# A five-engine graph-network kernel: every engine's round in another order, and another table of PSUM banks

## The chip, the cores and the metric

One core of one Trainium2 chip. The metric is the device time of one execution in microseconds; a smaller one is better. All data is fp32.

## The reference, cut to what matters

128 graphs with 128 nodes and 256 features each go through four residual layers. Every layer normalises x, applies relu, and adds its result to x:

```python
# L0, hypergraph convolution, twice, with a layer norm between; H = (adj != 0)
m = Be[:, :, None] * einsum('nce,nch->neh', H, x @ W1.T);  h = Dn[:, :, None] * einsum('nce,neh->nch', H, m)
h = layer_norm(relu(h + b1));  y = hypergraph_conv(h, adj, W2, b2);  y + x
# L1, graph attention: softmax over nodes of where(adj > 0.5, leaky(Wh1 + Wh2.T), -9e15), times Wh, then elu
# L2, three diffusion hops: transition = A*exp(leaky(sj + si)) / rowsum;  H = sum_k (transition^k X) Wk + bk; relu
# L3: w = softmax over nodes of rowsum((q k^T) * adj);  w * v
h = relu(layer_norm(x)); x = x + L0(h, adj);  ... x = x + L1(...);  x = x + L2(...);  x = x + L3(...)
```

## The kernel before

Four graphs form a group, and there are 32 groups. The kernel is a software pipeline over groups. In round i, group i+1 is prepared ("next": degrees, scaled incidence), group i goes through L0 and L1 ("front"), group i-1 through L2 ("mid"), group i-2 through most of L3 ("late"), and group i-3 is finished and stored ("tail"). Rounds 1 to 35 are the same function `body`; rounds 6 to 30 run as a hardware loop. Round 0 has its own list, `opening`.

Each engine has a `body` of its own, which is a list, written out by hand, of small named blocks. The order of the list is the order in which that engine works; between engines only semaphores count. A block waits for its inputs (`wait_ge`), and, where it writes a PSUM bank that another block used, for the reader of the old content (the calls of `wait` at a block's head).

TensorE's blocks of a round, in the order before: `front_w1(0)`; `front_att` 0 and 1, `mid_az` 2 and 3, `front_att` 2 and 3 of the round before; `front_w1` 1 and 2; `late_ak`; the transposes `mid_h2(0)`, `front_w1(3)`, `mid_h2(1)`; then `mid_p2` 0 to 3 mixed with the high passes `front_w2` and followed by `front_w2_low` and `front_sums`; `mid_b2`, `late_h3(0)`, `mid_p10` 0 and 1, `front_c2`, `tail_turn`, `next_s`, `mid_p10` 2 and 3, `late_h3(1)`, and then `late_vqk`, `mid_ap`, `next_d`, `front_b1`, `next_y`, `mid_az` and `front_mix`. Products of weights run in three passes of a split format (high times high, and two with the low parts); each block of six matmuls is one group of four graphs or one chunk.

ScalarE evacuates PSUM: `copy_u` (two activations for each of four chunks, hT and its high part), `elu_exp`, `relu_p0`, `copy_h2T`, `copy_p2`, `copy_p10`, `exp_edges`, `copy_vqk`, `tail_exp`. VectorE does the layer norms (`mid_ln2`, `late_ln3`, `front_ln1`: statistics, aggregation, subtraction), the low parts (`mid_low`, `late_low`, `front_low`, `y_low`), `mid_columns` (which writes sij from the last columns of the four p2 products), `front_variance`, `front_z`, `front_residual`, `next_degrees` (its last step, L1387, writes deg), `front_dots`, and the softmax steps. GpSimd does the adds that only touch SBUF and the power -0.5 of every variance (`rsqrt`). SP issues the DMAs in its own order: the loads of x and of the adjacency, the copy of the mask, the store.

`BANK` gives the PSUM banks (0 to 7, 512 fp32 columns each) of every named product: `"u": (1, 2, 0, 3)` puts the first chunk of u into bank 1. `late_ak(past)` works for the group of the round before, `tail_sum` to `tail_out` form the softmax over nodes by two small transpositions, `tail_row` and `tail_turn`.

## Time and profile before

| | us |
|---|---|
| median of 3 runs | 1414.67 (1414.25 to 1416.06) |
| profiled execution, its own time | 1416.56 |
| its span, first to last instruction | 1414.6 |

Busy time in the span: TensorE (PE) 1368.1 us, VectorE (DVE) 1270.0, ScalarE (ACT) 1053.9, GpSimd (POOL) 949.0. PEclk is the granted share of TensorE's clock; it is 1.00 in steady rounds and 0.985 in the mean over the span. Times in the rows are microseconds from the span's start. Matmuls are pipelined: the recorded end of one lies behind the start of the next, so the pace is read from start to start. The round shown in the rows begins for TensorE at 394.77 with `front_w1(0)`.

### The profile page before, as it was taken

How to read it: one execution, taken by the hardware profiler on the slowest of the kernel's cores; microseconds unless marked ns; L12 is line 12 of the kernel's file. 1: busy time of each engine (PE TensorE's matmuls, PEld its weight loads, DVE VectorE, ACT ScalarE, POOL GpSimd, SP SyncE). 2: the span in 40 equal slices, each digit the busy share in tenths (PEclk: the TensorE clock that was granted, in tenths of full speed). 3: DMA queues.
4: the chain of work that ended last, by engine and by line, in shares of the span. 5: the costliest groups of instructions: out<-in, count | busy, mean ns of one | idle time of the engine just before them, and what ended most of it. 6: DMA issues, size and time to landing. Idle time of an engine off the chain costs nothing.

```text
span 1414.6 us, 33539 instructions
## 1 busy us (share of the span) xinstructions
PE 1368.1 (97%) x8924; PEld 1249.5 (88%) x8924; DVE 1270.0 (90%) x5265; ACT 1053.9 (74%) x2345; POOL 949.0 (67%) x974
## 2 busy tenths in 40 slices
PE   7789999999999999999999999999999999999985
PEld 6678999999999999999999999999999999999975
DVE  6869999999999999999999999999999999999883
ACT  4556777877777887777887777788777788777664
POOL 5647666667766666866666776666686666677533
PEclk9889999999999999999999999999999999999997
DMA  4100111101111101111110111110111111011001
GB/s 127 31 28 27 38 38 54 53 24 44 52 37 52 52 23 46 50 52 37 52 46 28 44 52 37 52 52 22 44 52 52 37 52 44 30 44 37 31 31 53
DMA packets 75383, 62.15 MB, mean 44 GB/s; under 512 B 3013, under 2 KB 70985, under 8 KB 75338
## 3 DMA queue, kind: packets, MB, share of 16 engines
q1 hardware_dynamic: 75338, 61.63, 13.7%
q8 instruction: 19, 0.31, 0.1%
q14 instruction: 26, 0.21, 0.0%
HBM read 36.45 MB, written 16.78 MB: 38 GB/s over the span
## 4 chain that ended last, share of the span: by engine, by line
PE 92%; DVE 5%; issue 2%; ACT 1%; DMA 0%; POOL 0%; POOLq 0%; DVEq 0%; ACTq 0%; SPq 0%
PE ps L357 39%; PE ps L342 25%; PE ps L361 19%; PE ps L463 4%; PE ps L418 3%; DVE stats L1321 1%; DVE prod L1505 1%; DMA x_in<-in_x 0%; PE ps L619 0%; DVE h L1333 0%; DVE x L1468 0%; PE ps L615 0%; DVE x L1416 0%; DVE z L1461 0%; DVE el L1406 0%
## 5 line engine op out<-in xcount | busy, mean ns | idle before, releaser
L1100 POOL TENSOR_TENSOR x3n<-p,x 128x512 f32<-128x512 f32 x64 | 82.2, 1285 | 260.7 <-ACT p L853 260.7
L1060 POOL TENSOR_TENSOR hT_lo<-hT,hT_hi 128x512 fp32r<-128x512 f32 x126 | 161.3, 1302 | 56.8 <-ACT hT L795 42.1
L1040 POOL TENSOR_TENSOR rs<-var_e,neg_half 128x4 f32<-128x4 f32 x160 | 165.2, 1033 | 23.7
L774 ACT ACTIVATE p<-ps,rs 128x256 f32<-128x256 f32 (+1 forms) x256 | 136.6, 597 | 27.9 <-DVE sij L1422 27.6
L357 PE MATMUL ps<-wl_hi,h2T_hi 128*128 128x512 f32 (+1 forms) x512 | 148.5, 372 | 0.7 <-DVE x L1468 0.7
L342 PE MATMUL ps<-p,alT 128*128 128x256 f32 (+1 forms) x512 | 143.4, 383 | 0.5 <-DVE p L1446 0.5
L357 PE MATMUL ps<-wl_lo,h2T_hi 128*128 128x512 f32 (+1 forms) x512 | 132.3, 340 | 0.0
L361 PE MATMUL ps<-wl_hi,h2T_lo 128*128 128x512 f32 (+1 forms) x512 | 131.8, 339 | 0.0
L1321 DVE BATCH_NORM_STATS2 stats<-x 128x6 f32<-128x256 f32 x256 | 108.8, 425 | 5.7
L871 ACT ACTIVATE h3T_hi<-ps 128x512 fp32r<-128x512 f32 x64 | 38.3, 598 | 90.8 <-PE ps L463 86.9
L795 ACT ACTIVATE hT_hi<-ps,cols_sb 128x512 fp32r<-128x512 f32 x128 | 87.4, 683 | 21.8 <-PE ps L361 21.6
L361 PEld LDWEIGHTS ps<-wl_hi,h2T_lo 128*128 128x128 f32 x512 | 88.1, 190 | 11.6
L357 PEld LDWEIGHTS ps<-wl_lo,h2T_hi 128*128 128x128 f32 x512 | 88.4, 190 | 10.9
L1113 POOL TENSOR_TENSOR p<-p,bk 128x512 f32<-128x512 f32 x64 | 81.9, 1279 | 21.1 <-ACT p L774 21.1
L795 ACT ACTIVATE hT<-ps,cols_sb 128x512 f32<-128x512 f32 x128 | 87.5, 683 | 8.4 <-PE ps L361 4.8
L342 PEld LDWEIGHTS ps<-p,alT 128*128 128x128 f32 x512 | 85.1, 192 | 5.6 <-DVE p L1446 0.8
L1505 DVE CUSTOM_DVE_ANT_0 prod<-va,ps 128x256 f32<-128x256 f32 x256 | 90.0, 417 | 0.0
L357 PEld LDWEIGHTS ps<-wl_hi,h2T_hi 128*128 128x128 f32 x512 | 83.1, 191 | 6.4 <-issue 1.1
L1075 POOL TENSOR_TENSOR x<-x 128x512 f32<-128x512 f32 x64 | 80.6, 1281 | 11.7 <-ACT x L774 11.7
L463 PE MATMUL ps<-ident,h 128*128 128x128 f32 x512 | 79.4, 277 | 7.1 <-DVE h L1333 7.1
L357 PE MATMUL ps<-w_hi,hT_hi 128*128 128x258 f32 x512 | 85.8, 290 | 0.0
L357 PE MATMUL ps<-yT_hi,w_hi 128*128 128x512 f32 x256 | 85.4, 414 | 0.0
(188 smaller groups left out, 4604.9 us busy)
## 6 DMA issues: line engine op xcount, KB each, us to landing
x_in<-in_x SPq DMA_DIRECT2D x32, 512.0 KB, 3.4
out_x<-x SPq DMA_DIRECT2D x32, 512.0 KB, 3.2
adj_f<-in_adjT SPq DMA_DIRECT2D x32, 256.0 KB, 2.7
adj_m<-in_adjT SPq DMA_DIRECT2D x32, 256.0 KB, 2.9
adj_l<-adj_m SPq DMA_DIRECT2D x32, 256.0 KB, 2.4
vqk<-in_l_wk SPq DMA_DIRECT2D x3, 256.0 KB, 4.9
x<-in_w1T SPq DMA_DIRECT2D x1, 512.0 KB, 6.7
x<-in_w2T SPq DMA_DIRECT2D x1, 512.0 KB, 7.6
```

Source lines behind the costliest of these rows:

```text
L342: last = pe.matmul(dst, lhsT(c), rhs(c), start=(c == 0), stop=(c == chunks - 1))
L357: pe.matmul(dst, lhsT(a, c), rhs(b, c), start=(a == b == c == 0), stop=False)
L361: last = pe.matmul(dst, lhsT(1 - late, c), rhs(late, c), start=False, stop=(c == chunks - 1))
L463: last = pe.transpose(bank(name, b)[:, ((g % 2) * KC + c) * P:((g % 2) * KC + c + 1) * P], h[:, g, c * P:(c + 1) * P], ident[:])
L774: return act.activation(dst, src, ACT.Copy, scale=scale)
L795: act.activation(dst[:, hc, :], bank("u", hc), ACT.Relu, bias=cols_sb[:, 0, hc:hc + 1]).then_inc(S[ready], 1)
L1040: pool.tensor_tensor(rs[:, layer, :], var_e[:, layer, :], neg_half[:], ALU.pow).then_inc(done, G)
L1060: pool.tensor_tensor(hTs[1][:, hc, :], hT[:, hc, :], hTs[0][:, hc, :], ALU.subtract).then_inc(S["hT_lo"], 1)
L1100: pool.tensor_tensor(x3n[:, s], p0[:, s], x2[:, s], ALU.add).then_inc(S["x3_ready"], 2)
L1113: pool.tensor_tensor(p0[:, s, :], p0[:, s, :], bk[:].rearrange("p (a d) -> p a d", a=1) .broadcast_to((P, 2, D)), ALU.add).then_inc(S["p0b ...
L1321: dve.bn_stats(stats[:, layer, g, :], src[:, g, :]).then_inc(st, 1)
L1505: dve.tensor_tensor_reduce(prod[:, k, :], va[:, k * D:(k + 1) * D], bank("hp", b)[:, (g % 2) * D:(g % 2 + 1) * D], 1.0, 0.0, ALU.mult, ALU ...
```

## The change

Every engine's list is put into another order. No block is added, dropped or given to another engine. The table of banks is new, and with it the waits at the blocks' heads, since these belong to the bank's former user. In the opening, constant rows go to other banks accordingly.

TensorE: `mid_h2(0)` runs ahead of `late_ak`; the order among `mid_p2` and `front_w2` is other, with `mid_p2(3)` later; `tail_row` moves behind `late_h3(0)`; `next_s` moves ahead with `tail_turn` between its halves; `late_h3(1)`, `late_vqk` 0 and 1 and `next_d` run ahead of `mid_p10(3)`. ScalarE: `elu_exp(0)` and `relu_p0(1)` move from behind the next round's `copy_u(0)` to ahead of it; `tail_exp` moves behind `copy_h3T(0)`, `copy_s` ahead of `norm_x`, whose second half comes much later. GpSimd: `mask_edges` and both `add_bias` move behind the next round's `add_res0(0)`. VectorE: the counts and `binc` run ahead of `next_moments`, `tail_max` behind `front_variance`, `tail_sum` directly behind `tail_weights`. SP: `load_adj` and `store` ahead of `load_x`.

The diff, cut to its core:

```diff
-        BANK = {"u": (1, 2, 0, 3), "y": (1, 4), "s": (3, 4), "d": (2,), "c2": (5, 0), "b1": (0, 3), "att": (3, 5),
-                "h2": (7, 6), "p2": (4, 5, 6, 7), "p10": (6, 7, 5, 0), "b2": (4,), "z": (0, 1, 2, 3),
-                "ap": (4, 5, 6, 7), "az": (5, 4), "h3": (5, 7), "vqk": (3, 1, 2, 0), "ak": (1,),
-                "row": (2,), "turn": (1,), "yA": (3, 2), "hp": (2, 6)}
+        BANK = {"u": (1, 3, 0, 2), "y": (1, 3), "s": (4, 5), "d": (6,), "c2": (0, 7), "b1": (3, 2), "att": (2, 7),
+                "h2": (4, 6), "p2": (4, 5, 6, 7), "p10": (7, 5, 3, 7), "b2": (6,), "z": (0, 1, 2, 3),
+                "ap": (4, 5, 6, 7), "az": (5, 6), "h3": (4, 1), "vqk": (5, 4, 0, 2), "ak": (3,),
+                "row": (5,), "turn": (2,), "yA": (4, 0), "hp": (2, 0)}
...
             def load_x(r):
-                wait(sp, S["h0_ready"], r.front(G))
                 wait(sp, S["xb_ready"], r.front(G))
+                if not r.steady and r.i == 0:
+                    wait(sp, S["h0_ready"], r.front(G))
                 sp.dma_start(x_in[:], group(x, r.i + 1)).then_inc(S["x_loaded"], 16)
...
@@ -317,12 +316,13 @@
             def body(r):
                 past = r.later(-1)
                 if r.has_next:
+                    load_adj(r)
+                if past.has_tail:
+                    store(past)
+                if r.has_next:
                     load_x(r)
-                    load_adj(r)
                 if past.has_mid:
                     hand_adj(past)
-                if past.has_tail:
-                    store(past)
                 if past.has_front:
                     load_mask(past)
...
@@ -468,7 +463,9 @@
...
-                if g == 2:
+                if g == 0:
+                    wait(pe, S["h2T_lo"], r.mid(2))
+                elif g == 2:
                     wait(pe, S["h2T_lo"], r.mid(G))
                 pe.wait_ge(S["h2T_copied"], r.mid(2 * (g // 2) + 2))
...
@@ -480,22 +477,19 @@
...
                 if g == 0:
-                    wait(pe, S["p2_copied"], r.mid(3))
+                    wait(pe, S["p2_copied"], r.mid(G))
                 elif g == 1:
-                    wait(pe, S["p2_copied"], r.mid(G))
-                elif g == 2:
-                    wait(pe, S["x1_ready"], r.front(2))
-                    if not r.steady and r.i == GROUPS:
-                        wait(pe, S["h3T_lo"], r.late(2))
+                    wait(pe, S["wex_ready"], r.tail(G))
                 elif g == 3:
-                    wait(pe, S["x1_ready"], r.front(G))
+                    if not r.steady and r.i == GROUPS - 1:
+                        wait(pe, S["x1_ready"], r.front(G))
...
@@ -509,9 +503,10 @@
...
                 if g == 2:
-                    wait(pe, S["wex_ready"], r.tail(G))
+                    if not r.steady and r.i == 0:
+                        wait(pe, S["hT_ready"], r.front(G))
                 elif g == 3:
-                    wait(pe, S["hT_ready"], r.front(G))
+                    wait(pe, S["qak_ready"], r.tail(G))
                 pe.wait_ge(S["hT_hi"], r.front(G))
                 high_passes(*z_product(g))
...
@@ -528,12 +523,11 @@
...
             def mid_ap(r, g):
                 if g == 0:
-                    if not r.steady and r.i == 1:
-                        wait(pe, S["deg_ready"], r.next(G))
-                elif g == 1:
-                    wait(pe, S["p10_copied"], r.mid(3))
+                    wait(pe, S["vqk_copied"], r.late(2))
+                elif g == 2:
+                    wait(pe, S["gt_ready"], r.next(G))
                 elif g == 3:
-                    wait(pe, S["h3T_lo"], r.late(G))
+                    wait(pe, S["p10_copied"], r.mid(G))
...
@@ -544,19 +538,19 @@
...
                 if g == 0:
                     wait(pe, S["deg_ready"], r.next(G))
-                elif g == 1:
-                    if not r.steady and r.i in (GROUPS, GROUPS + 1,):
-                        wait(pe, S["wcol_ready"], r.tail(G))
+                    if not r.steady and r.i in (GROUPS - 1, GROUPS,):
+                        wait(pe, S["p10_copied"], r.mid(2))
                 elif g == 3:
-                    wait(pe, S["lz"], r.front(2))
-                    if not r.steady and r.i == GROUPS:
-                        wait(pe, S["p10_copied"], r.mid(G))
+                    wait(pe, S["lz"], r.front(G))
...
@@ -581,10 +573,8 @@
...
             def front_b1(r):
-                wait(pe, S["p10_copied"], r.mid(G))
-                wait(pe, S["vqk_copied"], r.late(1))
-                if not r.steady and r.i == 0:
-                    wait(pe, S["deg_ready"], r.next(G))
+                if not r.steady and r.i == 1:
+                    wait(pe, S["p10_copied"], r.mid(3))
                 pe.wait_ge(S["wh12_ready"], r.front(G))
...
             def late_ak(r):
-                wait(pe, S["hT_hi"], r.next(1))
+                wait(pe, S["hT_hi"], r.next(2))
                 pe.wait_ge(S["vqk_copied"], r.late(G))
...
             def tail_row(r):
+                wait(pe, S["p2_copied"], r.mid(2))
...
             def tail_turn(r):
+                wait(pe, S["z_ready"], r.front(3))
...
@@ -634,10 +622,10 @@
                 if r.has_front:
                     front_w1(r, 1)
                     front_w1(r, 2)
+                if r.has_mid:
+                    mid_h2(r, 0)
                 if past.has_late:
                     late_ak(past)
-                if r.has_mid:
-                    mid_h2(r, 0)
                 if r.has_front:
                     front_w1(r, 3)
                 if r.has_mid:
...
+                    front_w2(r, 1)
                     front_w2(r, 0)
                     front_w2(r, 3)
-                if r.has_tail:
-                    tail_row(r)
+                    front_w2_low(r, 0)
                 if r.has_mid:
                     mid_p2(r, 2)
                 if r.has_front:
-                    front_w2(r, 1)
+                    front_w2(r, 2)
                 if r.has_mid:
                     mid_p2(r, 3)
                 if r.has_front:
-                    front_w2(r, 2)
-                    front_w2_low(r, 0)
                     front_w2_low(r, 1)
                     front_w2_low(r, 2)
                     front_w2_low(r, 3)
@@ -665,53 +651,52 @@
                     front_sums(r, 1)
                     front_sums(r, 2)
                     front_sums(r, 3)
-                if r.has_mid:
-                    mid_b2(r)
                 if r.has_late:
                     late_h3(r, 0)
-                if r.has_mid:
+                if r.has_tail:
+                    tail_row(r)
+                if r.has_mid:
+                    mid_b2(r)
                     mid_p10(r, 0)
                     mid_p10(r, 1)
                 if r.has_front:
                     front_c2(r, 0)
                     front_c2(r, 1)
+                if r.has_next:
+                    next_s(r, 0)
                 if r.has_tail:
                     tail_turn(r)
+                if r.has_next:
+                    next_s(r, 1)
                 if r.has_front:
                     front_c2(r, 2)
-                if r.has_next:
-                    next_s(r, 0)
-                    next_s(r, 1)
-                if r.has_front:
                     front_c2(r, 3)
+                if r.has_late:
+                    late_h3(r, 1)
                 if r.has_mid:
                     mid_p10(r, 2)
                 if r.has_late:
-                    late_h3(r, 1)
+                    late_vqk(r, 0)
+                    late_vqk(r, 1)
+                if r.has_next:
+                    next_d(r)
                 if r.has_mid:
                     mid_p10(r, 3)
-                if r.has_late:
-                    late_vqk(r, 0)
-                if r.has_mid:
                     mid_ap(r, 0)
-                if r.has_next:
-                    next_d(r)
+                if r.has_front:
+                    front_b1(r)
                 if r.has_mid:
                     mid_ap(r, 1)
-                if r.has_late:
-                    late_vqk(r, 1)
-                if r.has_front:
-                    front_b1(r)
-                if r.has_mid:
                     mid_ap(r, 2)
                     mid_ap(r, 3)
                 if r.has_next:
                     next_y(r, 0)
                 if r.has_late:
                     late_vqk(r, 2)
+                if r.has_next:
+                    next_y(r, 1)
+                if r.has_late:
                     late_vqk(r, 3)
-                if r.has_next:
-                    next_y(r, 1)
                 if r.has_mid:
                     mid_az(r, 0)
                 if r.has_front:
...
@@ -896,10 +881,6 @@
                 if r.has_front:
                     copy_u(r, 0)
                 if past.has_front:
-                    elu_exp(past, 0)
...
-                if past.has_front:
...
@@ -922,45 +901,50 @@
...
                     copy_h3T(r, 0)
+                if r.has_tail:
+                    tail_exp(r)
                 if r.has_mid:
                     exp_edges(r)
                     copy_p10(r, 0)
                     copy_p10(r, 1)
                 if r.has_next:
-                    norm_x(r, 0)
                     copy_s(r, 0)
                     copy_s(r, 1)
-                    norm_x(r, 1)
+                    norm_x(r, 0)
                 if r.has_front:
                     centre_logits(r, 0)
                 if r.has_late:
                     copy_h3T(r, 1)
-                if r.has_mid:
-                    copy_p10(r, 2)
-                if r.has_front:
-                    centre_logits(r, 1)
-                if r.has_mid:
-                    copy_p10(r, 3)
                 if r.has_tail:
                     weigh(r, 0)
+                if r.has_front:
+                    centre_logits(r, 1)
+                if r.has_mid:
+                    copy_p10(r, 2)
                 if r.has_late:
                     copy_vqk(r, 0)
+                    copy_vqk(r, 1)
+                if r.has_front:
+                    front_centre(r, 0)
+                if r.has_mid:
+                    copy_p10(r, 3)
+                if r.has_next:
+                    norm_x(r, 1)
+                if r.has_front:
+                    leaky_part(r, 0)
                 if r.has_tail:
                     weigh(r, 1)
-                if r.has_late:
-                    copy_vqk(r, 1)
-                if r.has_front:
-                    front_centre(r, 0)
-                    leaky_part(r, 0)
+                if r.has_front:
                     leaky_part(r, 1)
                 if r.has_next:
                     copy_yT(r, 0)
                 if r.has_front:
                     softmax(r, 0)
                     softmax(r, 1)
-                    front_centre(r, 1)
                 if r.has_late:
                     copy_vqk(r, 2)
+                if r.has_front:
+                    front_centre(r, 1)
                 if r.has_next:
                     copy_yT(r, 1)
                 if r.has_late:
@@ -973,6 +957,10 @@
                     copy_h1T(r, 1)
                 if r.has_mid:
                     relu_p0(r, 0)
+                if r.has_front:
+                    elu_exp(r, 0)
+                if r.has_mid:
+                    relu_p0(r, 1)
 
...
@@ -1148,17 +1135,21 @@
                 past = r.later(-1)
                 if r.has_front:
                     add_res0(r, 0)
+                if past.has_mid:
+                    mask_edges(past)
                 if past.has_front and (r.steady or past.i != 0):
                     front_scale1(past)
                 if past.has_mid:
-                    add_bias(past, 1)
+                    add_bias(past, 0)
                 if past.has_tail:
                     add_x4(past, 0)
                     add_x4(past, 1)
+                if past.has_mid:
+                    add_bias(past, 1)
+                if past.has_next and (r.steady or past.i != 0):
+                    add_xb(past, 1)
                 if r.has_front:
                     add_res0(r, 1)
-                if r.has_next:
-                    add_xb(r, 0)
                 if past.has_mid:
                     add_x3(past, 0)
                     add_x3(past, 1)
...
+                    front_scale0(r)
                 if r.has_next:
                     next_scale(r)
-                    shift_x(r)
-                if r.has_front:
-                    front_scale0(r)
                 if r.has_late:
                     late_scale(r)
                 if r.has_next:
-                    add_xb(r, 1)
-                if r.has_mid:
-                    add_bias(r, 0)
-                    mask_edges(r)
+                    shift_x(r)
+                    add_xb(r, 0)
 
             def opening(r):
...
@@ -1584,30 +1571,28 @@
             def body(r):
                 ahead = r.later(1)
                 if r.has_next:
-                    next_moments(r)
-                if r.has_tail:
-                    tail_sum(r)
+                    next_count(r)
+                    next_inverse(r)
                 if r.has_mid:
                     mid_low(r, 1)
+                if r.has_next:
+                    next_binc(r)
                 if r.has_late:
                     late_ln3(r, 0)
+                if r.has_next:
+                    next_moments(r)
+                if r.has_mid:
+                    mid_columns(r)
+                if r.has_late:
+                    late_ln3(r, 1)
+                if r.has_front:
+                    front_variance(r)
                 if r.has_tail:
                     tail_max(r)
-                if r.has_next:
-                    next_count(r)
-                    next_inverse(r)
-                if r.has_mid:
-                    mid_columns(r)
-                if r.has_next:
-                    next_binc(r)
                 if r.has_late:
-                    late_ln3(r, 1)
-                if r.has_front:
-                    front_variance(r)
+                    late_low(r, 0)
                 if r.has_tail:
                     tail_norm(r)
-                if r.has_late:
-                    late_low(r, 0)
                 if r.has_front:
                     front_z(r, 0)
                     front_z(r, 1)
...
```

The rest of the diff is small moves among VectorE's softmax steps, `tail_exp` and the squares taken from their old places on ScalarE, banks of the opening's constant rows, waits at heads that belong to the banks, and, in the opening, `front_b1` without its wait for deg, `second_rows` behind `next_d`, and one `elu_exp(0)` at the end of ScalarE's list.

## Rows read from the trace of the kernel before

**Rows 1.** The page's first part: busy us (share of the span) x instructions.
```profile
PE 1368.1 (97%) x8924; PEld 1249.5 (88%) x8924; DVE 1270.0 (90%) x5265; ACT 1053.9 (74%) x2345; POOL 949.0 (67%) x974
```

**Rows 2.** Stretches, second round and a steady one: start:end, length, busy, PEclk, DMA.
```profile
56.30:103.70 47.40, 40.94 (x239) 35.51 (x238) 36.13 (x152) 26.24 (x60) 23.14 (x24) 0.89 0.04 12
391.47:433.33 41.86, 41.86 (x281) 38.53 (x280) 38.98 (x164) 32.71 (x74) 29.43 (x30) 1.00 0.14 44
```

**Rows 3.** Timeline, PE, one steady round: start, length, line, operation, out<-in, shape, count.
```profile
397.67 1.03 PE L342 MATMUL ps<-p,alT 128*128 128x256 f32 x4
...
402.73 1.00 PE L342 MATMUL ps<-vqk,adj_l 128*128 128x64 f32 x8
403.56 0.61 PE L463 MATMUL ps<-ident,h 128*128 128x128 f32 x4
...
405.75 0.49 PE L357 MATMUL ps<-wl_hi,h2T_hi 128*128 128x258 f32 x2
...
411.47 0.40 PE L361 MATMUL ps<-wl_hi,h2T_lo 128*128 128x258 f32 x2
411.74 0.75 PE L357 MATMUL ps<-w_hi,hT_hi 128*128 128x258 f32 x4
412.33 0.64 PE L357 MATMUL ps<-w_lo,hT_hi 128*128 128x258 f32 x4
412.81 2.11 PE L361 MATMUL ps<-w_hi,hT_lo 128*128 128x258 f32 x16
...
420.23 0.22 PE L619 MATMUL ps<-ident,wex 4*128 4x4 f32 x1
420.38 0.70 PE L342 MATMUL ps<-z,gt 128*128 128x256 f32 x2
...
423.99 0.71 PE L357 MATMUL ps<-wl_hi,h2T_hi 128*128 128x512 f32 x2
...
425.46 0.51 PE L357 MATMUL ps<-wl_hi,h3T_hi 128*128 128x384 f32 x2
```

**Rows 4.** Timeline of ACT in the same round; in brackets, idle time before and its releaser.
```profile
396.69 0.63 ACT L853 ACTIVATE p<-p 128x512 f32<-128x512 f32 x1 [0.75 <-DVE p L1478]
397.23 0.67 ACT L795 ACTIVATE hT<-ps,cols_sb 128x512 f32<-128x512 f32 x1
...
399.78 0.63 ACT L853 ACTIVATE p<-p 128x512 f32<-128x512 f32 x1 [0.47 <-DVE p L1478]
401.01 0.58 ACT L867 ACTIVATE ps<-ps 128x512 f32<-128x512 f32 x1 [0.60 <-DVE el L1406]
401.55 0.69 ACT L795 ACTIVATE hT<-ps,cols_sb 128x512 f32<-128x512 f32 x1
402.13 0.68 ACT L795 ACTIVATE hT_hi<-ps,cols_sb 128x512 fp32r<-128x512 f32 x1
...
411.50 0.18 ACT L800 ACTIVATION_READ_ACCUMULATOR wex<-ps,wsm 4x1 f32 x1
```

**Rows 5.** Timeline of DVE in the same round.
```profile
398.81 0.88 DVE L1478 SCALAR_TENSOR_TENSOR p<-ps,rsum,p 128x256 f32<-128x256 f32 x2 [0.17 <-PE ps L342]
...
405.17 0.69 DVE L1225 SCALAR_TENSOR_TENSOR h2T_lo<-ps,h2T_hi 128x512 fp32r<-128x512 f32 x1
...
410.87 0.27 DVE L1545 TENSOR_REDUCE wsm<-ps 4x1 f32<-4x128 f32 x1
...
412.19 0.17 DVE L1422 TENSOR_TENSOR sij<-ps,rs 128x8 f32<-128x8 f32 x1
...
413.02 0.35 DVE L1359 TENSOR_SCALAR_CACHE_REDUCE binc_T<-inc_T,cnt 128x128 f32<-128x128 f32 x1
...
414.09 0.88 DVE L1321 BATCH_NORM_STATS2 stats<-x3n 128x6 f32<-128x256 f32 x2
...
418.22 1.66 DVE L1461 SCALAR_TENSOR_TENSOR z<-ps,rs,bw 128x256 f32<-128x256 f32 x4
...
423.72 0.16 DVE L1387 SCALAR_TENSOR_TENSOR deg<-ps,deg 128x4 f32<-128x4 f32 x1
```

106 lines of the change are left out of this document (46 added, 60 removed).

## Prediction

> **What bounds the kernel now.** I read the page first: TensorE is busy for 97% of the span, VectorE for 90%, ScalarE and GpSimd for far less [rows 1]. Then the table of stretches. A steady round takes 41.86 us, and TensorE is busy in all of it at the full granted clock; VectorE works 38.98 us, ScalarE 32.71, GpSimd 29.43 [rows 2]. So a steady round is as long as TensorE's own list of matmuls, plus what it loses to waits that are too short to show as idle time, because a matmul's recorded end overlaps the next start. Those are found in the timeline of one round, in the distance from start to start. There I see two. The block at 411.74 (the high passes of front_w2 of group 2) needs 0.59 us for four matmuls where its other half needs 0.48, and starts 0.03 late: it waited for ScalarE's exponential, whose accumulator read ends at 411.68 [rows 3, 4]. That wait costs 0.14 us, and its work restarts, in effect, 0.17 us after the releaser's end (411.68 to 411.74 + 0.11). I use 0.17 as **the price of a release** below. The other loss sits round the 4x4 transposition (tail_turn) at 420.23, whose successor starts 0.15 later where its own work is 4 columns [rows 3]; that is the shape, not a wait, since its input is long ready. Everything else runs at the pace of the loads and columns. VectorE has 2.9 us of slack in a round, most of it the short gaps between dependent small steps.
>
> The start is different: in the second round (56.30 to 103.70) TensorE works 40.94 of 47.40 us at a mean clock of 0.89 [rows 2].
>
> **What the change cannot alter.** The same matmuls, activations and vector operations are issued with the same shapes; no DMA is added or dropped. So TensorE's sum stays and only waits can move: the round can gain at most the 0.14 us above, plus whatever of the start and the end is shortened. Against that stand all the new waits. I went through each engine's new list, placed each block at the end of the one ahead of it, and looked for waits whose releaser comes later than TensorE's arrival. All but a few have between 0.15 and 2 us in hand; the following do not.
>
> **Term A, the wait of late_ak.** In the new table "ak" lies in bank 3, which u's second block uses, so late_ak waits for the second copy_u (both activations) of the round. TensorE now reaches it after front_w1(2) and the four transposes of mid_h2(0): front_w1(2) ends at 402.73, eight matmuls of ak take 0.83 (402.73 to 403.56), so four transposes at that pitch take 0.42 and it arrives at 403.15 [rows 3]. ScalarE's new order ahead of that copy is relu_p0(1), copy_u(0), elu_exp(1), copy_u(1). relu_p0(1) starts at 399.78, because it waits for VectorE's two p0 steps, that start at 398.81, and these for the matmuls of 397.67 [rows 3 to 5]; all of these stay where they are. From there: relu to the next start 0.54 (396.69 to 397.23), copy_u(0) two activations of 0.58 (401.55 to 402.13), elu_exp 0.54 at most (401.01 to 401.55), copy_u(1) 0.58 and the second activation's 0.68 to its end [rows 4]. 399.78 + 0.54 + 1.16 + 0.54 + 0.58 + 0.68 = 403.28, with the release 403.45: a stall of 0.30 us. If elu_exp follows as tightly as the others it is 0.06 less. Taken: 0.25; bounds 0 and 0.35. In the old order copy_u(0) ran in the gap ahead of elu_exp(0), where ScalarE was idle, so that nothing waited for it. Behind the wait stand ak, front_w1(3), mid_h2(1) and all of mid_p2.
>
> A second chain ends at nearly the same place. mid_p2(0) now shares bank 4 with the transposes of h2 and waits at its start for VectorE's mid_low(0), which ends at 405.17 + 0.69 = 405.86, released 406.03; TensorE came there at 405.75 plus 0.08 (the first fast matmul after a slow transposition is recorded that much early) [rows 3, 5]: 0.20. It is not added, since a stall at late_ak pushes mid_p2(0) by as much; but it means that at least 0.2 us is lost here even where term A is small.
>
> **Term B, the degrees ahead of late_vqk(0).** The wait was there already, with 1.4 us in hand: deg is made by 423.72 + 0.16 = 423.88, TensorE arrives at 425.46 [rows 3, 5]. Now mid_p2(3), from which VectorE's chain starts (its last columns give sij), comes later in TensorE's list, and late_vqk(0) earlier. TensorE's way from the end of mid_p2(3) (411.74, less the 0.03) to late_vqk(0) was 13.72 us. Out of it go front_w2(2) with its stall (1.07, 411.74 to 412.81), a quarter of the low passes (16 in 2.11, so 0.5) and mid_p10(3) (423.99 to 425.46, 1.39 to 1.47); one transposition of 0.1 comes in: 10.8 us. VectorE's way: sij starts 0.27 after mid_p2(3) leaves off (a matmul's recorded end plus 0.11, as at 398.81 after 397.67 + 1.03), then from 412.19 to 423.88 it took 11.69, of which the four binc steps (413.02 to 414.09, 1.07) now run earlier; 10.62, and the release 0.17 [rows 3, 5]: 11.06. The stall is 0.16 to 0.26. The moved tail_max (0.27) costs nothing in it: it comes to stand with late_low(0) and tail_norm in the stretch ahead of z at 418.22, in which VectorE waits for GpSimd's power of the variance anyway; without that cover it would add its 0.27 [rows 5]. Taken: 0.20; bounds 0 and 0.35.
>
> **The wait removed.** The exponential's bank moves to p2(1)'s, and mid_p10(1) waits for it, 6 us later than before. tail_max now stands behind the second layer norm, so wex comes at about 417.7 and TensorE at 418.0: 0.1 to 0.2 in hand. Gain 0.14, or 0 if that is gone.
>
> **Edits at no cost.** The 4x4 transposition moves between the two halves of next_s; the second half must wait for ScalarE's copy of p10(1) until about 421.0, when TensorE gets there anyhow (bounds -0.1 and +0.1). On GpSimd mask_edges stands behind add_res0, which waits for norm_x(0): al is ready some 2.5 us later, 2 us ahead of mid_ap(0). add_bias and add_xb move likewise inside 12 us of free GpSimd time. On SP's queue the load of x goes from ahead of load_adj to behind it and the store; load_adj waits for the penalties at the very start of a TensorE round, and next_moments, which wants x, now comes after the counts, binc and a layer norm, an estimated 10 us after the load lands; hand_adj and load_mask keep their places behind the store. front_b1 loses its old waits and meets wh12 within 0.1 us (0 to 0.1).
>
> **Start and end.** In the opening front_b1 no longer waits for deg, about -0.7 us; in the second round one mid_ap more lies behind front_b1, +0.4 to +0.9; in the last rounds tail_max stands behind one more layer norm, +0.5 to +1. Sum: nothing, within 2 us either way.
>
> **Sum.** A 0.25 + B 0.20 - 0.14 = +0.31 us a round, 0.30 taken. 32 rounds have a front part; the opening, the two rounds after it and the last are not bounded by TensorE alone, so 28 count: +8.4 us. The profiled execution took 1416.56 us (span 1414.6 and 2.0 around it), 1.9 above the median; on the median of 1414.67 the sum gives 1423.1. Its own range, with 0.1 to 0.45 a round, is 1417.5 to 1427.5.
>
> **The rivals.** (1) *Faster: the new waits are covered.* A vanishes if ScalarE gains 0.25 us on the way to copy_u(1) and VectorE 0.2 to mid_low(0); B if VectorE's chain is 0.2 shorter than I add up. Then only the 0.14 gain stays, 28 x 0.14 = 4: **1410.7**. Decided at a stall below 0.14 a round in all. For it: each is a difference of two sums of ten rows. Against it: all these durations stand in rows, and two chains end at mid_p2(0). (2) *No change*: one of the two terms holds and is smaller than counted; 0.0 to 0.1 a round, **1416**. (3) *More waits*: the waits with 0 to 0.15 us in hand (wex in mid_p10(1), wh12 in front_b1, p10 in next_s, the copy of vqk in mid_ap(0)) fall too, 0.2 to 0.3 a round more: **1430**. (4) *The clock.* In the second round the mean clock of 0.89 costs 0.11 x 47.40 = 5.2 us [rows 2]. If the new order has TensorE idle less there, that comes back (forecast 1418); if a steady round lost the clock as well, each would cost some 5 us, over 1500. Against the last: rounds with 0.14 us of stall and the gaps of tail_turn kept 1.00 [rows 2].
>
> On this the Trainium skill ("TensorE: Matmul & The Clock Gate", section "A second HAM failure mode: psum-queue depth-cycling") warns that cycling through PSUM banks can leave pauses between groups of matmuls by which the clock goes back and forth. Applied here it would be the last case of rival 4. The trace of before does not bear it out in steady rounds.
>
> **How the numbers follow.** Chances: forecast with its own range 0.57, rival 1 0.17, rival 2 0.15, rival 3 0.10, the clock lost in steady rounds 0.01. A measurement of this kernel can tell 0.2%, 2.8 us. Faster (below 1411.8) 0.17, within 0.16, slower 0.67. The range that should hold 8 in 10 takes in rival 1 and most of rival 3: 1411 to 1430.
>
> **What would show it.** A: in the steady round the ak matmuls start 0.2 to 0.3 us after the transposes ahead of them leave off, released by copy_u's activation. B: the first matmul of late_vqk(0) is released by deg. The block front_w2(2) runs its four matmuls in 0.48. The stretch of a steady round reads 42.1 to 42.25 at clock 1.00. Rival 1 reads 41.7 there; a round of 41.86 or less with neither wait would make the prediction wrong.

## The result, and where the time went

The changed kernel takes **1440.1 us** (median of 3 runs, 1438.4 to 1441.8) against 1414.67 before: a ratio of 1.0169, 95% interval 1.0154 to 1.0185. The forecast was 1423.0 in a range of 1411 to 1430. Slower was right, the size was not: +25.4 us, three times the +8.4 that were forecast.

The first part of the changed kernel's page, to be set against [rows 1], has TensorE busy for 21 us more (with the same matmuls; short stalls lie under their recorded ends) and VectorE for 27 us more with the same 5265 instructions.

```profile
PE 1389.1 (96%) x8924; PEld 1248.0 (87%) x8924; DVE 1297.4 (90%) x5265; ACT 1034.4 (72%) x2345; POOL 953.1 (66%) x974
```

The table of stretches (columns as in [rows 2]), second round and a steady one:

```profile
64.31:108.37 44.06, 37.36 (x231) 32.08 (x230) 33.72 (x138) 26.97 (x62) 24.42 (x25) 0.96 0.04 11
656.20:698.84 42.64, 42.45 (x281) 38.38 (x280) 40.05 (x164) 32.01 (x74) 29.56 (x30) 1.00 0.14 43
```

The steady round is 42.64 us in place of 41.86, at a granted clock of 1.00 in both. VectorE works 40.05 in it, 1.07 more than in [rows 2]. The profiled span is 1439.9, 25.3 longer than before. Cut at each round's first copy of u (ScalarE), the difference splits so: the 25 rounds from the seventh on +19.5 (25 x 0.78), rounds 3 to 6 +1.6, the first two +2.8, the first copy itself 1.9 later in this execution, the end -0.6. So most of it lies in the steady rounds.

TensorE's round of the changed kernel, which begins at 656.20, at the places where the distance from start to start is longer than the matmuls need (columns as in [rows 3]):

```profile
664.17 0.60 PE L458 MATMUL ps<-ident,h 128*128 128x128 f32 x4
664.92 1.10 PE L342 MATMUL ps<-vqk,adj_l 128*128 128x64 f32 x8 [0.16 <-issue]
665.83 0.71 PE L357 MATMUL ps<-yT_hi,w_hi 128*128 128x512 f32 x2
...
667.67 0.49 PE L357 MATMUL ps<-wl_hi,h2T_hi 128*128 128x258 f32 x2
...
681.92 0.61 PE L342 MATMUL ps<-binc_T,inc_T 128*128 128x129 f32 x4
682.46 0.22 PE L607 MATMUL ps<-ident,wex 4*128 4x4 f32 x1
682.70 0.71 PE L342 MATMUL ps<-binc_T,inc_T 128*128 128x129 f32 x4
...
685.48 0.62 PE L361 MATMUL ps<-wl_hi,h2T_lo 128*128 128x512 f32 x2
685.94 0.53 PE L357 MATMUL ps<-wl_hi,h3T_hi 128*128 128x384 f32 x2
...
689.88 0.59 PE L342 MATMUL ps<-p,alT 128*128 128x257 f32 x2
690.48 0.65 PE L416 MATMUL ps<-ident,wh 128*128 128x128 f32 x4
...
696.15 0.59 PE L342 MATMUL ps<-p,alT 128*128 128x256 f32 x2
696.65 1.13 PE L342 MATMUL ps<-pT,h1r 128*128 128x128 f32 x8
```

- late_ak (664.92): the four transposes need 0.43, the next start is 0.75 behind. That is 0.32, and with the slower first steps of the block **0.39** against before.
- next_s, second half (682.70): beyond one small matmul's 0.11, the place round the 4-row tile (tail_turn, 682.46) takes 0.33, and 0.23 before [rows 3]: **+0.10**. The tile is the same; what is new is a wait, shown below.
- late_vqk(0) (685.94): it starts on time, **0.03** at most.
- front_b1 (690.48): two matmuls of 257 columns need 0.44, the distance is 0.60; with the steps behind **0.22**.
- front_mix (696.65): two of 256 columns need 0.43, the distance is 0.50; with the steps behind **0.14**.
- The wait for the exponential in front_w2(2) is gone, **-0.14**.

The sum is 0.74 of the 0.78. The term of late_ak is the least sure: from the transposes of mid_h2(0) to mid_p2(0) (664.17 to 667.67) the round takes 3.50 us, and the same four blocks took 3.02 before (402.73 to 405.75 [rows 3]), 0.48 less. The wait in next_s is for ScalarE's copy of p10(1), the second of these two activations:

```profile
681.34 1.23 ACT L759 ACTIVATE p<-ps,rs 128x512 f32<-128x512 f32 x2
```

It ends at 682.57, and next_s goes on 0.13 later. In the 23 rounds between 300 and 1300 us that distance is 0.128 or 0.129 each time, while the distance from the tile varies between 0.24 and 0.27.

Two of the terms, front_b1 and front_mix, 0.36 together, are stalls for VectorE at blocks that were hardly counted. What makes VectorE late there is this, in its timeline and GpSimd's:

```profile
690.00 0.42 DVE L1500 TENSOR_TENSOR wh<-wh12r,rs 128x8 f32<-128x8 f32 x1
...
695.50 0.61 DVE L1508 TENSOR_TENSOR rz<-rz,rs 128x2 f32<-128x2 f32 x1
...
696.95 0.39 DVE L1508 TENSOR_TENSOR rz<-rz,rs 128x2 f32<-128x2 f32 x1
```

```profile
689.11 1.29 POOL L1100 TENSOR_TENSOR p<-p,bk 128x512 f32<-128x512 f32 x1
...
694.81 1.27 POOL L1100 TENSOR_TENSOR p<-p,bk 128x512 f32<-128x512 f32 x1
696.06 1.26 POOL L1081 TENSOR_TENSOR xb<-x_in,b2m 128x512 f32<-128x512 f32 x1
```

A product of 2 columns takes 0.61 us, where a step of that size takes 0.16 elsewhere. Each of the three long products ends 22 or 23 ns after the GpSimd add that was running when it began (689.11 + 1.29 = 690.40; 694.81 + 1.27 = 696.08; 696.06 + 1.26 = 697.32). No other short step of VectorE varies like this in the steady rounds; what these share is that both inputs are tensors in SBUF. The groups of instructions by line show it as a mean (the column behind the busy time is the mean ns of one); first the kernel before, then the changed one:

```profile
L1513 DVE TENSOR_TENSOR wh<-wh12r,rs 128x8 f32<-128x8 f32 x32 | 11.1, 348 | 4.3
L1521 DVE TENSOR_TENSOR rz<-rz,rs 128x2 f32<-128x2 f32 x64 | 11.1, 173 | 6.7
```

```profile
L1508 DVE TENSOR_TENSOR rz<-rz,rs 128x2 f32<-128x2 f32 x64 | 29.6, 463 | 6.7
...
L1500 DVE TENSOR_TENSOR wh<-wh12r,rs 128x8 f32<-128x8 f32 x32 | 14.1, 440 | 4.3
```

The Trainium skill ("SBUF — State Buffer", section "Who interferes with whom") states such a rule: a VectorE instruction with two SBUF inputs contends with a GpSimd instruction that reads SBUF, the ports that the two engines share are an exclusive lock, and the order of issue decides which of them is blocked. The three rows fit it; the runs below ask whether it sets the time.

### The profile page after: what moved, and what is told of

Same layout as the page of the kernel before. It is cut to its first block, busy times and chain, and to the rows that moved or that the text cites. A ratio compares the mean times of both kernels' runs of the same rounds, so it can differ in the third digit from the quotient of the medians.

```text
span 1439.9 us, 33329 instructions
## 1 busy us (share of the span) xinstructions
PE 1389.1 (96%) x8924; PEld 1248.0 (87%) x8924; DVE 1297.4 (90%) x5265; ACT 1034.4 (72%) x2345; POOL 953.1 (66%) x974
## 4 chain that ended last, share of the span: by engine, by line
PE 91%; DVE 5%; issue 2%; POOL 1%; ACT 0%; DMA 0%; POOLq 0%; DVEq 0%; ACTq 0%
PE ps L357 38%; PE ps L342 26%; PE ps L361 19%; PE ps L458 4%; PE ps L416 3%; DVE stats L1308 1%; DVE prod L1492 1%; DVE h L1320 0%; DVE z L1448 0%; PE ps L607 0%; PE ps L383 0%; DVE x L1455 0%; PE ps L602 0%; POOL rs L1029 0%; DMA adj_f<-in_adjT 0%
## 5 line engine op out<-in xcount | busy, mean ns | idle before, releaser
L759 ACT ACTIVATE p<-ps,rs 128x256 f32<-128x256 f32 (+1 forms) x256 | 133.3, 573 | 141.4 <-DVE sij L1409 140.6
L357 PE MATMUL ps<-wl_hi,h2T_hi 128*128 128x512 f32 (+1 forms) x512 | 143.4, 362 | 0.5 <-DVE h2T_lo L1212 0.5
L342 PE MATMUL ps<-p,alT 128*128 128x256 f32 (+1 forms) x512 | 137.9, 382 | 0.5 <-ACT vqk L759 0.4
L342 PEld LDWEIGHTS ps<-p,alT 128*128 128x128 f32 x512 | 90.0, 191 | 9.5 <-ACT vqk L759 0.8
L1095 POOL TENSOR_TENSOR res<-xb,h 128x512 f32<-128x512 f32 x64 | 82.2, 1286 | 11.1 <-POOL xb L1081 10.1
L458 PEld LDWEIGHTS ps<-ident,h 128*128 128x128 f32 x512 | 63.9, 147 | 23.5 <-DVE h L1320 8.0
L357 PE MATMUL ps<-w_hi,hT_hi 128*128 128x258 f32 x512 | 82.8, 284 | 0.3 <-ACT hT L780 0.3
```

Source lines behind the costliest of these rows:

```text
L342: last = pe.matmul(dst, lhsT(c), rhs(c), start=(c == 0), stop=(c == chunks - 1))
L357: pe.matmul(dst, lhsT(a, c), rhs(b, c), start=(a == b == c == 0), stop=False)
L458: last = pe.transpose(bank(name, b)[:, ((g % 2) * KC + c) * P:((g % 2) * KC + c + 1) * P], h[:, g, c * P:(c + 1) * P], ident[:])
L759: return act.activation(dst, src, ACT.Copy, scale=scale)
L1095: pool.tensor_tensor(res0[:, s], xb[:, s], h0[:, s], ALU.add).then_inc(S["res0_ready"], 2)
```

## The experiments

Theory L: VectorE's wh12 and rz products stand still until GpSimd's running add ends, and TensorE waits for them at front_b1 and front_mix; late_ak's stall is a separate one, from ScalarE's order and the banks. Rival W: GpSimd's order is indifferent, and all of the loss is the waits of the bank table and of ScalarE's order. The kernel before ran beside each of three sets of four experiments, in the order below except that the run with the first wait alone belongs to the third set: 1416.4 us (7 runs), 1415.9 (12 runs) and 1415.9 (18 runs, 1412.4 to 1419.3). A ratio is to the set beside it, the range behind it is the 95% interval, and "round" is the length of a steady round.

**GpSimd's list put back.** Edit, in the changed kernel: GpSimd's `body` as before (the diffs are cut to their core).

```diff
+                if r.has_next:
+                    add_xb(r, 0)
...
+                    add_xb(r, 1)
+                if r.has_mid:
+                    add_bias(r, 0)
+                    mask_edges(r)
```

> The changed kernel with GpSimd's list alone put back to that of before (mask_edges, both add_bias and add_xb at their old places); everything else as changed. Theory L (VectorE's wh12 and rz products, which read two SBUF operands, stand still until GpSimd's running add has ended): in a steady round the two rz products fall from 0.60 and 0.39 us to 0.16 and wh12 from 0.42 to about 0.23; front_b1's stall of 0.23 and front_mix's of 0.14 go, and since the seam comes earlier on VectorE, late_ak's stall falls from 0.39 to about 0.25: round 42.64 - 0.5 = 42.1, time 1424 to 1430. Rival W (GpSimd's order is indifferent, the loss is the waits that the bank table and ScalarE's order bring): the products keep 0.4 to 0.6 or their length does not matter, round 42.6, time 1439 to 1441.

Measured: **1683.9 us**, 1.190 (1.188 to 1.193), rounds of 51.2. That is neither theory's time, and the run tests neither of them, because it brought a long wait of its own, as SyncE's queue and then GpSimd's timeline show:

```profile
862.13 0.37 SPq L295 DMA_DIRECT2D adj_f<-in_adjT  x1
862.79 0.40 SPq L305 DMA_DIRECT2D out_x<-x  x1
863.38 0.37 SPq L301 DMA_DIRECT2D x_in<-in_x  x1
```

```profile
868.37 1.26 POOL L1083 TENSOR_TENSOR xb<-x_in,b2m 128x512 f32<-128x512 f32 x1 [11.82 <-DMA x_in<-in_x]
```

The old list has add_xb(0) in the middle of the seam, the changed one loads x only behind load_adj, which waits for the penalties. GpSimd stands for 11.8 us with the steps for x3 and hT_lo queued behind it. The lists of GpSimd and SyncE are one change; half of it undone is worse than either kernel. The products still follow the adds: wh12, which no add covers now, takes 0.17 in every round after the opening, and the first rz product 0.78 to 0.80, up to the end of an add.

**ScalarE's seam put back.** Edit: `elu_exp(0)` and `relu_p0(1)` behind the next round's `copy_u(0)`, and the `elu_exp(0)` at the end of the opening's list taken out.

```diff
                if past.has_front:
+                    elu_exp(past, 0)
+                if past.has_mid:
+                    relu_p0(past, 1)
+                if past.has_front:
                     elu_exp(past, 1)
```

> The changed kernel with ScalarE's elu_exp(0) and relu_p0(1) back behind the next round's copy_u(0), so that the copy for which late_ak waits ends about 1.1 us earlier; GpSimd's list as changed. Theory L: late_ak's stall of 0.39 goes, but wh12 and rz stay long (0.42, 0.60, 0.39) and front_b1 and front_mix keep 0.2 to 0.4 between them: round 42.2 to 42.4, time 1429 to 1434. Rival W: with the wait gone, what is left is the 0.10 of tail_turn against the 0.14 gained, round 41.9, time 1418 to 1421.

Measured: **1435.9 us**, 1.0137 (1.012 to 1.0154), round 42.49. Both missed, W by more. late_ak's stall is gone, but mid_p2(0) takes its place: it starts 0.52 after the four transposes' start, 0.09 behind their end and, counted with its slower first steps, 0.19 late, released by VectorE's mid_low(0). That is the second chain of the prediction, which is hidden while late_ak stalls. front_b1 and front_mix keep their stalls. The profiled spans differ by 5.0 us: 25 steady rounds bring 3.5 and the first two rounds 4.0, and the end takes 2.1 back. In the first two, `elu_exp(0)` at the end of the opening's list no longer stands ahead of `copy_u(0)`; in the changed kernel ScalarE stood there for 4.9 us, waiting for VectorE.

**GpSimd's new list in the kernel before.** Edit: that list alone.

```diff
+                if past.has_mid:
+                    mask_edges(past)
...
-                    add_bias(past, 1)
+                    add_bias(past, 0)
```

> The kernel before with nothing but GpSimd's list of the change. Theory L: VectorE's rz and wh12 products get longer here too (rz from 0.16 to 0.3 to 0.6 us in part of the places), though no wait of TensorE was added; VectorE has 2.9 us of slack in a round, so that only what lies at front_b1 and front_mix is lost, 0 to 0.4 us a round: time 1415 to 1426. Rival W: GpSimd's order is indifferent, 1413.5 to 1416, the products as in the kernel before.

Measured: **1452.6 us**, 1.0263 (1.0246 to 1.028), round 43.23. W falls: one engine's list with 12 us of free time costs 36 us. L's mechanism holds, its price was far too low. VectorE, GpSimd and TensorE in turn:

```profile
693.60 1.23 DVE L1511 TENSOR_TENSOR wh<-wh12r,rs 128x8 f32<-128x8 f32 x1
```

```profile
693.53 1.27 POOL L1075 TENSOR_TENSOR x<-x 128x512 f32<-128x512 f32 x1
```

```profile
694.98 0.40 PE L418 MATMUL ps<-ident,wh 128*128 128x128 f32 x2 [0.89 <-DVE wh L1511]
```

The add began 0.07 us ahead of the product, which then took all but that of the add's length, and so it is in every steady round.

**One SBUF operand.** Edit: the products per graph, with a column operand and an accumulated output.

```diff
-                dve.tensor_tensor(rz[:, s], rz[:, s], rs[:, 1, s], ALU.mult)
+                for g in (2 * b, 2 * b + 1):
+                    dve.tensor_scalar(rz[:, g:g + 1], rz[:, g:g + 1], rs[:, 1, g:g + 1], None, ALU.mult, ALU.add,
+                                      accum_out=unread2[:, 0, g:g + 1])
```

> The changed kernel with all lists as changed; only the rz and wh12 products are written per graph with a column operand and an accumulated output (eight instructions with one SBUF tensor in place of three with two). Theory L: none of these stands still while GpSimd adds, each takes some 0.1 to 0.17 us; the stalls of front_b1 and front_mix fall by more than half, against up to 0.4 us of extra instructions on VectorE: round 42.1 to 42.4, time 1425 to 1434. Rival W: the same work in more instructions, no shorter in sum, time 1440 to 1446.

Measured: **1440.9 us**, 1.0179 (1.0162 to 1.0196), round 42.75. The time is W's, the rows are L's: each of the instructions takes 0.21 us in every round, adds or not, and front_mix's stall is gone. But wh12 is now four steps in a row, 0.62 us (688.08 to 688.70) in place of 0.42, and front_b1's stall grows from 0.22 to 0.43. The form escapes the block and costs as much.

**The adds wait for the products.** Edit, in the changed kernel: two waits on GpSimd.

```diff
                 if past.has_mid:
+                    if past.has_front:
+                        pool.wait_ge(S["wh12_ready"], past.front(G))
                     add_bias(past, 0)
...
                 if past.has_mid:
+                    if past.has_front:
+                        pool.wait_ge(S["rz_ready"], past.front(G))
                     add_bias(past, 1)
```

> The changed kernel with every list as changed, and two waits more on GpSimd: the add of the first bias half does not start before wh12 is made, that of the second half (with add_xb and add_res0 behind it) not before the second rz product is made. Theory L (VectorE's products with two SBUF operands stand still until GpSimd's running add ends, and TensorE waits for them): wh12 falls from 0.42 to 0.16 us, the rz products from 0.60 and 0.39 to 0.16; front_b1's stall falls from 0.23 to under 0.05 and front_mix's 0.14 goes, while late_ak keeps its 0.39, which does not hang on them: round 42.64 - 0.35 = 42.3, time 1428 to 1432. Rival M (the products' length is hidden on VectorE, the stalls come from the order of VectorE's own list): the products get short, the round stays at 42.6, time 1438 to 1442.

Measured: **1429.4 us**, 1.0102 (1.0086 to 1.0119), round 42.28, as L has it. VectorE, then GpSimd:

```profile
852.91 0.17 DVE L1504 TENSOR_TENSOR wh<-wh12r,rs 128x8 f32<-128x8 f32 x1
...
858.22 0.16 DVE L1512 TENSOR_TENSOR rz<-rz,rs 128x2 f32<-128x2 f32 x1
...
859.22 0.16 DVE L1512 TENSOR_TENSOR rz<-rz,rs 128x2 f32<-128x2 f32 x1
```

```profile
853.30 1.27 POOL L1100 TENSOR_TENSOR p<-p,bk 128x512 f32<-128x512 f32 x1 [1.26 <-DVE wh L1504]
...
859.51 1.27 POOL L1100 TENSOR_TENSOR p<-p,bk 128x512 f32<-128x512 f32 x1 [1.95 <-issue]
```

The work is the same, its order too; GpSimd waits 1.26 and 1.95 us more, and the kernel is 10.7 us faster (ratio 1.0102 in place of 1.0169, and the intervals lie apart). Neither front_b1 nor front_mix stalls any longer; late_ak keeps its 0.3.

**The first wait alone.** Edit: without the wait for `rz_ready`.

> The changed kernel with the first of the two waits of r7_adds_wait alone (the first bias add after wh12); the adds beside the rz products run as in the changed kernel. If the two stalls are separate, front_b1's 0.23 goes, front_mix's 0.14 stays: round 42.42, time 1433 to 1435. If the delayed adds move off the rz products by themselves, or VectorE's earlier start makes the rz products miss them, the round is 42.3 as with both waits: 1429 to 1431.

Measured: **1431.4 us**, 1.0106 (1.0088 to 1.0124), round 42.43: 0.21 for front_b1's stall, and the 0.15 from here to 42.28 for front_mix's. wh12 takes 0.17, the rz products 0.60 and 0.39. The stalls are separate (the time lies 2 us below what was expected for such a round, and the intervals of this kernel and the one with both waits overlap; that they are separate rests on the rounds and the rows).

**Both: the adds wait, and ScalarE's seam is back.**

> The same two waits on GpSimd and, besides, ScalarE's elu_exp(0) and relu_p0(1) back behind the next round's copy_u(0). If the round's loss is the sum of separate stalls (late_ak 0.39, front_b1 0.23, front_mix 0.14, the 4x4 transposition 0.10, less 0.14 gained), then both fixes add: what is left is the wait of mid_p2(0) for mid_low(0) that stands behind late_ak's (0.19 when late_ak's is gone), so the round is 42.15 and the time 1423 to 1427, some 2 us of it gained at the start, where elu_exp(0) no longer holds up copy_u(0). If they hang together on one chain, the second fix brings nothing: 1428 to 1432.

Measured: **1420.4 us**, 1.0032 (1.002 to 1.0044), round 41.98: the fixes add, and a little more than was expected (42.15). What is left against 41.86 is mostly mid_p2(0)'s wait, here 0.12 in place of 0.19, and the 0.10 in next_s less the 0.14.

**late_ak's waits in another order.** Edit, in the changed kernel:

```diff
-                wait(pe, S["hT_hi"], r.next(2))
                 pe.wait_ge(S["vqk_copied"], r.late(G))
                 pe.wait_ge(S["adj_l_loaded"], r.loads(r.i - 2))
+                wait(pe, S["hT_hi"], r.next(2))
```

> The changed kernel with late_ak's three waits in another order: the one for copy_u, which comes last in time, is also the last in the code. Theory R (TensorE's sequencer works out the values of the next two waits only after the first one is released, and that adds 0.1 us to the release): late_ak's matmuls start some 0.17 us after copy_u's end in place of 0.28, round 42.54, time 1436 to 1439. Rival (the release takes 0.28 whatever stands behind it): no difference, 1439 to 1442.

Measured: **1435.4 us**, 1.0136 (1.0114 to 1.0157), round 42.51, -0.12, as theory R has it. The copy ends at 833.22 + 0.70 = 833.92 and the first matmul of ak starts 0.15 later; in the changed kernel it is 0.24 (663.99 + 0.69 to 664.92), and the matmul behind it comes later too (0.155 in place of 0.132). The two rows of this run, ScalarE's and TensorE's:

```profile
833.22 0.70 ACT L780 ACTIVATE hT_hi<-ps,cols_sb 128x512 fp32r<-128x512 f32 x1
```

```profile
833.43 0.60 PE L458 MATMUL ps<-ident,h 128*128 128x128 f32 x4
834.07 0.63 PE L342 MATMUL ps<-vqk,adj_l 128*128 128x64 f32 x4
```

In the changed kernel's trace TensorE's sequencer (the part of the engine that handles waits) works on the values for the other two waits at 664.72 and 664.83, behind the copy's end at 664.68.

**The two gaps of the kernel before.** Edit, in the kernel before: `front_w2_low(0)` ahead of `front_w2(2)`, and the 4x4 transposition over all rows.

```diff
-                pe.transpose(bank("turn")[:, 0:G], wex[0:G, :], ident[0:G, 0:G])
+                pe.matmul(bank("turn")[:, 0:G], wex[:], ident[:, 0:G])
```

> The kernel before with its two known gaps on TensorE attended to: front_w2_low(0) runs ahead of front_w2(2), so that the wait for the exponential has 0.5 us more, and the transposition of the weights reads all 128 rows of wex (zeros behind the fourth) in place of a 4-row tile. If the 0.23 us round the 4x4 transposition is the change of the tile's shape, it falls to 0.05 or less, and with the wait's 0.14 the round is 41.86 - 0.3 = 41.55, time 1405 to 1408. If the 0.23 is the price of any small matmul there, only the wait's 0.14 goes: 1410 to 1412. If VectorE or ScalarE takes over: 1414.

Measured: **1440.5 us**, 1.0184 (1.0165 to 1.0204): 25 us slower, where 7 to 10 faster was expected. Both gaps are closed, and the fourth to the sixth round (3 to 5 in the next expectation, which counts from zero) take 41.35, 41.67 and 41.66. The seventh takes 42.79, and so does each one after it. VectorE's product in the sixth and the seventh round, then GpSimd's adds:

```profile
259.61 0.17 DVE L1514 TENSOR_TENSOR wh<-wh12r,rs 128x8 f32<-128x8 f32 x1
...
301.34 1.29 DVE L1514 TENSOR_TENSOR wh<-wh12r,rs 128x8 f32<-128x8 f32 x1
```

```profile
258.40 1.28 POOL L1113 TENSOR_TENSOR p<-p,bk 128x512 f32<-128x512 f32 x1 [0.40 <-ACT p L774]
259.63 2.53 POOL L1075 TENSOR_TENSOR x<-x 128x512 f32<-128x512 f32 x2
...
300.10 1.28 POOL L1113 TENSOR_TENSOR p<-p,bk 128x512 f32<-128x512 f32 x1 [0.37 <-ACT p L774]
301.34 2.51 POOL L1075 TENSOR_TENSOR x<-x 128x512 f32<-128x512 f32 x2
```

In the sixth round the product starts 0.02 us ahead of the add, in the seventh a few ns behind it, and then it lasts as long as the add. The loop stays so for the remaining rounds, and TensorE waits for the product at front_b1, 0.87 us a round. In the kernel before, VectorE's product and GpSimd's adds stand so in a steady round:

```profile
428.09 0.23 DVE L1513 TENSOR_TENSOR wh<-wh12r,rs 128x8 f32<-128x8 f32 x1
```

```profile
428.26 2.52 POOL L1075 TENSOR_TENSOR x<-x 128x512 f32<-128x512 f32 x2
```

The product starts 0.17 us ahead of the add of x: that is all that keeps it out of this.

**The same with one wait on GpSimd.** Edit: as above, and the second bias add waits for wh12.

> The kernel before with the two gaps of TensorE attended to, as in c1_before_two_gaps, and one wait more on GpSimd: the add of the second bias half, which stands behind the power of the variance, does not start before wh12 is made. Theory L: in c1 the add started 0 to 4 ns ahead of the product from the seventh round on, and the product took 1.30 us in place of 0.17; with the wait it stays at 0.17 in every round, the rounds keep the 41.66 of c1's rounds 3 to 5 or less, and the time is 1416 - 28 x 0.25 = 1406 to 1410. Rival: TensorE, 0.3 us a round earlier, waits for VectorE's list at another place: rounds of 41.8 or more, 1413 or more.

Measured: **1408.7 us** (6 runs), **0.9954** (0.9938 to 0.997): faster than both kernels. wh12 takes 0.17 from the second round on, the steady round 41.72. Now the rz products meet the delayed adds (0.33 and 0.39), at front_mix without a stall. The two gaps give 0.25 a round: 0.13 for the wait, and 0.12 for the tile, since its 128-row form is two matmuls and takes 0.22 where the tile took 0.35. Half of that is lost again at the last product of mid_ap, which now starts 0.06 behind the end of VectorE's low part of h3T and runs 0.12 late. So the rival of the expectation came in part. Against the next run, which has the same start, the 25 steady rounds bring 3.3 us.

**That wait alone in the kernel before.**

> The kernel before with the one wait on GpSimd alone, without the two gaps closed. wh12 falls from 0.23 to 0.17 us; VectorE has slack there and TensorE has no stall at front_b1, so theory L expects no difference: 1414 to 1417. A gain of more than 3 us would say that the add cost the kernel before something that its trace does not show.

Measured: **1411.0 us** (10 runs), 0.9975 (0.9962 to 0.9989). No difference was expected, and 4.9 us came. The steady round is 41.85, as good as before; the first three rounds are 5.9 us shorter, of which the second brings 3.8 and the third 1.6. In the kernel before wh12 takes 1.27 and 1.30 us in these two, with this wait 0.17. So the kernel before paid for the block in its start, which its trace shows and which was not looked for. But the second round differs in the granted clock too, 1.00 here (the last but two of the columns) and 0.89 before [rows 2]:

```profile
57.81:101.36 43.55, 37.29 (x243) 32.36 (x242) 34.74 (x152) 26.30 (x60) 23.13 (x24) 1.00 0.05 13
```

The clock of that round does not go with the block: it is 0.96 in the run with two gaps closed, where wh12 is long there, 0.96 in the one with both waits, where it is short, and 1.00 in the one with the first wait alone. So the third round's gain, at 1.00 in both kernels, fits the block (the product alone is 1.1 shorter); how much of the second round's 3.8, and so of the 4.9, is the block's and how much the clock's stays open.

**The 128-row transposition in the best version of the changed order.**

> r8_adds_wait_scalar_back with the transposition of the weights over all 128 rows (zeros behind the fourth). The gaps round it, 0.32 us against one small matmul's 0.11, fell to nothing in c1. If they do here too, the round is 41.98 - 0.3 = 41.7, time 1408 to 1412. If VectorE's chain bounds the round by then, 41.85 or more, 1414 or more.

Measured: **1420.6 us**, 1.0037 (1.0023 to 1.0051), round 41.98: nothing gained. The gap is closed on its near side, and the wait of next_s fills it:

```profile
842.51 0.28 PE L607 MATMUL ps<-ident,wex 128*128 128x4 f32 x2
842.86 0.71 PE L342 MATMUL ps<-binc_T,inc_T 128*128 128x129 f32 x4
```

The second half of next_s starts 0.35 behind the small block, and again 0.13 behind the end of ScalarE's copy of p10(1). In the changed order that copy sets the start, whichever form the small block has.

## Why the prediction failed, step by step

- **The step that failed** is "add_bias and add_xb move likewise inside 12 us of free GpSimd time", under the edits at no cost. Free time on the engine that is moved was taken for the whole price. The adds came to run over VectorE's wh12 and rz products and blocked them for 0.2 to 0.45 us each. Behind them stand front_b1, bounded at 0 to 0.1 and measured 0.22, and front_mix, not named at all, 0.14. The two are 0.36 a round, nearly half of the 0.78; the run with the two waits took just these back (42.64 to 42.28).
- **The sign that was there.** [rows 5] were read at single instances of each step. The mean of wh12 in the kernel before, 348 ns against 170 for sij of the same shape [rows 5], and its 1.30 us in the third round, would have shown the block. (In the kernel before the long ones are those of the first three rounds and the last; a steady one takes 0.23.)
- **Term A was right in kind and too small**: 0.25 forecast, 0.39 measured (up to 0.48 if the whole stretch is charged to it). ScalarE's chain was right: relu_p0(1) to the end of copy_u(1) was reckoned at 3.50 us and took 3.45 (661.23 to 664.68). What was off is the price of a release, 0.17: with two more waits behind the late one it costs 0.12 more than without them, as the run with the waits in another order shows. The second chain to mid_p2(0) was right: with late_ak's stall gone, 0.12 to 0.19 appear there.
- **Term B did not come**: 0.20 forecast, 0.03 measured. VectorE's way from sij (675.27) to deg (685.79) took 10.52, forecast 10.62; TensorE's, from 674.98, took 10.96 in place of 10.8, of which 0.10 is the wait in next_s. (The 13.72 in the prediction's sum is counted from 411.74; with the 0.03 taken off, as it says, it is 13.75, and the way 10.85.) The two ends of this difference were each right within 0.2, which was the whole term.
- **The wait removed** gave its 0.14. The wait of **next_s** for the copy of p10(1), with tail_turn between the halves, was put at nothing, with +0.1 as a bound, and cost that.
- **Start and end** were put at 0 within 2 us: the first two rounds cost 2.8, the end gave 0.6. The term left out is `elu_exp(0)` at the end of ScalarE's opening list; with ScalarE's seam as before, these rounds are 4.0 shorter. The 2.8 hold a gain as well: the second round's clock is 0.96 in place of 0.89, which by the reckoning of the prediction's fourth rival is worth some 3.4 us (0.11 x 47.40 less 0.04 x 44.06, an estimate). The clock of that round differs between the runs, so this gain is not shown to be the new order's.
- **The rivals.** The third one (more waits) named two of the waits that fell, wh12 in front_b1 and p10 in next_s, and gave 0.2 to 0.3 for them, where 0.32 was measured. It had no reason for wh12 to be late, left out front_mix and the start, and stopped at 1430. Of the fourth, its last case fell: the steady rounds keep a clock of 1.00, and the rule that the prediction set beside it (the Trainium skill, "TensorE: Matmul & The Clock Gate", section "A second HAM failure mode: psum-queue depth-cycling") is not borne out by these rounds.

The sum in the form of the prediction is 0.39 + 0.03 + 0.22 + 0.14 + 0.10 - 0.14 = 0.74 a round; times 28 that is 20.7, and with the start 23.5 of the 25.4.

## What to carry to other kernels

When an engine's list is reordered, look not only at who waits for the moved step but at what it will run beside: for every step of VectorE with two SBUF inputs on a path that matters, note which GpSimd instruction covers it, before and after. A group whose mean is twice that of its neighbours of the same shape is the place to look, and a wait on the engine with free time (1.3 to 2 us of GpSimd here) can win back time: here it was 10.7 us. A tuned loop can sit right beside such a place, 0.17 us in the kernel before, so that a gain of 0.25 us a round elsewhere pushed it in; such a gain should be tried together with the wait that guards against it.

## What the hardware showed

- A product on VectorE with two SBUF inputs and two columns takes 0.16 us alone. Beside a GpSimd add of 128x512 it takes up to 0.62 in the steady rounds of the changed kernel, 0.80 with GpSimd's list put back, and 0.97 in the opening of the kernel before. One with eight columns takes 0.17 alone and up to 1.30. A prolonged product ends 13 to 27 ns after the add, in all runs. The form with one SBUF tensor and an accumulated output (0.21 us) was never prolonged.
- The order of the two starts decides. A product recorded 20 ns or more ahead of the add was not held by it, and one recorded behind it was; between 4 and 9 ns ahead both occurred (0.17 once, with the two gaps closed; 1.30 twice, in the last rounds of that kernel and of the kernel before). A loop can stay on the bad side for all of its remaining rounds.
- A released wait on TensorE with two more waits behind it costs 0.12 us more than as the last of the three. late_ak's first matmul starts 0.24 us after the recorded end of ScalarE's releasing activation in the first case and 0.15 in the second; in next_s, with one wait behind the late one, it is 0.13.
- A 4-row tile between 128-row ones costs 0.35 us of TensorE in the kernel before, where a small matmul takes 0.11. Over 128 rows with zeros the same result takes two matmuls and 0.22 us, the pace of other small matmuls.
